# Filter layer 2, inverse row transform and whitening in four 64x64 parts of the array, in pairs of banks

## The reference, cut to what matters

```python
x = whiten(x) * gamma + beta             # per pixel a 64x64 product
h = layer_norm(x) * g1 + b1              # LN1
xf = rfft2(h, axes=(1, 2), norm='ortho') # 56 x 29 frequencies
o1 = relu(xf (complex) * w1 + b1)        # block diagonal, 8 blocks of 8: filter layer 1
o2 = softshrink(o1 (complex) * w2 + b2)  # filter layer 2, then shrink by 0.01
h = irfft2(o2) + h_input                 # inverse row transform, inverse column transform
y = gelu(layer_norm(h) @ mw1 + mb1) @ mw2 + mb2 + h    # LN2 and MLP, hidden 256
```

## Time and profile before

| | |
|---|---|
| median of the runs | 790.2 us (789.82 to 791.2) |
| the profiled execution's own time | 792.25 us |
| its span (first to last instruction) | 790.5 us |
| busy PE / DVE / ACT / POOL | 736.1 / 566.4 / 390.5 / 287.0 us |
| mean granted TensorE clock | 0.981 of full speed |
| one step in the middle (441.3 to 520.2 us) | 78.9 us |

### The profile page before, as it was taken

How to read it: one execution, slowest core, us unless ns; L and a number is a source line. 1 busy time by engine, 2 the same in 40 slices (tenths; PEclk the granted TensorE clock), 3 DMA queues, 4 the chain that set the end, 5 groups by cost and what they waited for, 6 DMA issues and landing times.

```text
span 790.5 us, 24576 instructions
## 1 busy us (share of the span) xinstructions
PE 736.1 (93%) x10489; PEld 495.7 (63%) x10489; DVE 566.4 (72%) x1845; ACT 390.5 (49%) x709; POOL 287.0 (36%) x158
## 2 busy tenths in 40 slices
PE   6988999788789999999999999999999999899887
PEld 5986557666566667666766677567766666557333
DVE  4566998869978587858785878587858794942741
ACT  0012004643746564656465646564656445645365
POOL 7000000771763356235623562356235624552000
PEclk9898999999999999999999999999999999989999
DMA  9974000203000400040004000300000000001001
GB/s 242 245 173 145 3 2 19 68 2 83 3 2 25 118 27 2 27 115 27 2 29 114 26 3 30 111 27 6 30 27 26 8 31 25 26 14 34 22 32 66
DMA packets 11069, 39.83 MB, mean 50 GB/s; under 512 B 1954, under 2 KB 2082, under 8 KB 9506
## 3 DMA queue, kind: packets, MB, share of 16 engines
q1 hardware_dynamic: 10962, 38.27, 17.1%
HBM read 25.42 MB, written 12.85 MB: 48 GB/s over the span
## 4 chain that ended last, share of the span: by engine, by line
PE 74%; DVE 17%; ACT 5%; issue 3%; DMA 0%; ACTq 0%; DVEq 0%
PE psum L1192 11%; PE psum L1183 10%; PE psum L1120 7%; PE psum L1131 6%; PE psum L1160 5%; PE psum L880 4%; PE psum L1047 4%; PE psum L1087 3%; DVE stats L626 3%; ACT o_g L1363 3%; PE psum L1173 3%; PE psum L931 3%; PE psum L1201 3%; DVE n L671 3%; PE psum L1104 3%
## 5 line engine op out<-in xcount | busy, mean ns | idle before, releaser
L1386 ACT ACTIVATE hid<-psum,hbias 128x448 f32<-128x448 f32 x224 | 123.9, 635 | 78.6 <-PE psum L1183 78.6
L459 POOL TENSOR_TENSOR p_y<-layer,clamped 128x512 f32<-128x512 f32 x64 | 75.9, 1186 | 90.9 <-DVE clamped L733 90.9
L438 POOL TENSOR_TENSOR hbuf<-hbuf,prm 128x896 f32<-128x896 f32 (+1 forms) x29 | 53.5, 1847 | 148.2 <-PE psum L1071 148.2
L1183 PE MATMUL psum<-n2T,mw1s 64*128 64x448 f32 x448 | 103.0, 577 | 3.0 <-ACT o_g L1363 2.2
L1192 PE MATMUL psum<-hid,prm 128*64 128x448 f32 x448 | 96.3, 552 | 3.3 <-DVE oslice L742 3.2
L433 POOL TENSOR_TENSOR rbuf<-ybuf,prm 128x512 f32<-128x512 f32 (+2 forms) x10 | 32.5, 3246 | 157.2 <-DVE hbuf L852 129.1
L727 DVE TENSOR_TENSOR layer<-psum,prm 128x512 f32<-128x512 f32 x64 | 40.4, 631 | 41.0 <-PE psum L1120 41.0
L1120 PEld LDWEIGHTS psum<-w2s,o_g 128*64 128x64 f32 x1856 | 60.1, 138 | 15.3 <-issue 11.2
L1131 PEld LDWEIGHTS psum<-cst,p_y 128*128 128x128 f32 x512 | 61.2, 192 | 10.6 <-issue 6.3
L1120 PE MATMUL psum<-w2s,o_g 128*64 128x64 f32 x1856 | 66.1, 224 | 1.6 <-ACT o_g L1363 1.2
L1131 PE MATMUL psum<-cst,p_y 128*128 128x112 f32 x512 | 66.6, 277 | 0.5 <-DVE layer L727 0.5
(11 more groups left out here) (138 smaller groups left out, 1338.0 us busy)
## 6 DMA issues: line engine op xcount, KB each, us to landing
xin<-x_dram SPq DMA_DIRECT2D x8, 1568.0 KB, 8.7
out_dram<-oslice SPq DMA_DIRECT2D x112, 112.0 KB
ybuf<-x_dram SPq DMA_DIRECT2D x2, 1568.0 KB, 18.4
fbuf<-x_dram SPq DMA_DIRECT2D x2, 1568.0 KB, 21.5
xin<-x_dram SPq DMA_DIRECT2D x4, 392.0 KB, 5.6
n<-x_dram SPq DMA_DIRECT2D x1, 1568.0 KB, 26.2
n<-x_dram SPq DMA_DIRECT2D x4, 392.0 KB, 18.9
prm<-params_dram SPq DMA_DIRECT2D x1, 742.0 KB, 4.1
```

The lines of the kernel that those rows point to most:

```text
L459: nc.gpsimd.tensor_tensor(yk, a, b, ALU.subtract).then_inc(y_ready, 1)
L1183: nc.tensor.matmul(t[:, 0:4 * ROWS], mw1s[C * v:C * v + C, HH * m:HH * m + HH], n2T[C * v:C * v + C, s % 2, :], start=True, stop=True).the ...
L1386: nc.scalar.activation(hid[:, s % 2, m, v, :], bank[CH_MLP[i].bank[k]][:, 0:4 * ROWS], ACT.Gelu, bias=hbias[:, m:m + 1]).then_inc(c_act, 1)
```

## The change

1. `layer_2`: instead of 128 input rows, each product takes the 64 rows of one image and 64 of the 128 outputs; one call fills two banks (one for each image, `b`) for `L2_KH[k]` frequency rows: 64, 64, 64 and 40 instructions. A pair still has 116 products. Before, a chunk was one half of the frequencies of both images in a bank; now the partition halves of a bank are the halves of the frequencies. The weights `w2s`, `mask2`, `fb2` shrink accordingly. POOL reads and writes chunks in the new arrangement.
2. `inv_w`: each product takes the 58 rows of half the channels (`h`) and 64 columns of weights; the real and imaginary halves (`s`) are accumulated: 8 products of 112 columns where there were 2, 256 instructions a pair. A call fills two banks, and it waits for all eight chunks (`y_ready` 8) where the first four calls waited for four.
3. `whiten_two(i, q)`: chunks 1+2, 3+4, 5+6 of pairs 2 to 7 in four parts, 64 columns each: 64 instructions for two chunks, where there were 16. `ev_whiten` writes every second column group.
4. Order on PE: slice 0 becomes `mlp_in` first half, `whiten_two(1)`, `mlp_in` second half, `transpose_n(1)`, `whiten_two(2)`. Slices 1 to 4 have five places; two chunks of layer 2 stand together. The last `inv_w` moves behind `mlp_in(5)`, `inv_h(0)` behind `dft_h(0)`, and `inv_h(3)` ahead of `dft_h(2)`.
5. Order on DVE: `multiply_rstd(i-1,1)` moves from ahead of the whitening evictions to behind them; layer 2 chunks are emptied two at a time, statistics in between; `ln2_stats` 0 and 1 move ahead of `ev_inv_h` 4 and 5. Order on ACT: the same five places, `ev_inv_w` two at a time.

```diff
-X_BESIDE = {1: [[0], [], [1], []], 2: [[2], [], [3], []], 3: [[4], [5], [6], []]}
+X_BESIDE = {1: [0, 1], 2: [2, 3], 3: [4, 5, 6]}
...
-                    if behind:
-                        multiply_rstd(i - 1, 1)
                     whitened_next(0, 1, 2)
...
+                    def second_product():
+                        if behind:
+                            multiply_rstd(i - 1, 1)
+
                     slice_(0, lambda: whitened_next(3, 4), lambda: whitened_next(5),
-                           lambda: whitened_next(6), lambda: stats_next(0))
-                    slice_(1, lambda: ev_layer_2(i, [0]), lambda: (ev_layer_2(i, [1]), stats_next(1)),
-                           lambda: ev_layer_2(i, [2]), lambda: (ev_layer_2(i, [3]), stats_next(2)))
-                    slice_(2, lambda: (ev_layer_2(i, [4]), stats_next(3)),
-                           lambda: (ev_layer_2(i, [5]), stats_next(4)),
-                           lambda: ev_layer_2(i, [6]), lambda: (ev_layer_2(i, [7]), stats_next(5)))
+                           lambda: whitened_next(6), second_product)
+                    slice_(1, lambda: ev_layer_2(i, [0, 1]), lambda: stats_next(0),
+                           lambda: ev_layer_2(i, [2, 3]), lambda: stats_next(1, 2))
+                    slice_(2, lambda: ev_layer_2(i, [4, 5]), lambda: stats_next(3),
+                           lambda: ev_layer_2(i, [6, 7]), lambda: stats_next(4, 5))
...
+                def whiten_two(i, q):
...
+                    for j in range(8):
+                        at = (4 + 8 * q + j) * RP
+                        for b in range(2):
+                            for v in range(2):
+                                rows = slice(C * v, C * v + C)
+                                last = nc.tensor.matmul(bank[WHITEN[2 * q + 1 + v]][C * b:C * b + C, j * C:j * C + C],
+                                                        xT[rows, at + C * b:at + C * b + C], wy[rows, rows], start=True, stop=True)
...
+                def layer_2(i, k, js):
+                    if k == 0 and i < PAIRS - 1:
+                        pe.wait_ge(whitened, (i + 1) * 7 + 6)
+                    t = [free_b(i, L2 + 2 * k + b) for b in range(2)]
+                    for j in js:
+                        for half in range(2):
+                            at = (half * KF + 8 * k + j) * KR
+                            for b in range(2):
+                                one = nc.tensor.matmul(t[b][C * half:C * half + C, j * C:j * C + C], o_g[C * b:C * b + C, at:at + C],
+                                                       w2s[C * b:C * b + C, C * half:C * half + C], start=True, stop=True)
...
+                def inv_w(i, k, js):
+
+                    pe.wait_ge(y_ready, i * 8 + 8)
+                    t = [free_b(i, INVW + 2 * k + h) for h in range(2)]
+                    for j in js:
+                        for s in range(2):
+                            for d in range(2):
+                                for h in range(2):
+                                    rows = slice(C * h, C * h + KR)
+                                    one = nc.tensor.matmul(t[h][C * d:C * d + C, j * 112:j * 112 + 112],
+                                                           y_v[rows, CH // 2 * s + 4 * k + j, C * d:C * d + C],
+                                                           cc("invw")[rows, 112 * s:112 * s + 112],
+                                                           start=(s == 0), stop=(s == 1), skip_group_check=True)
...
+                    def spectral_slice(s, one, two, three, four, five):
+
+                        if behind:
+                            mlp_in(i - 1, s)
+                        one()
+                        if behind:
+                            mlp_out(i - 1, s - 1)
+                        two()
+                        three()
+                        if behind:
+                            transpose_n(i - 1, s + 1)
+                        four()
+                        five()
+                        if behind:
+                            turn_out(i - 1, s - 1)
...
-                    slice_(0, whiten_next)
-                    slice_(1, and_x(1, lambda j: layer_2(i, j)))
-                    slice_(2, and_x(2, lambda j: layer_2(i, 4 + j)))
-                    slice_(3, and_x(3, lambda j: inv_w(i, [j])))
-                    slice_(4, lambda j: inv_w(i, [4 + j]))
+                    if behind:
+                        mlp_in(i - 1, 0, (0,))
+                    whiten_next(1)
+                    if behind:
+                        mlp_in(i - 1, 0, (1,))
+                        transpose_n(i - 1, 1)
+                    whiten_next(2)
+                    for s in (1, 2):
+                        a, b = 2 * s - 2, 2 * s - 1
+                        mid = L2_KH[b] // 2
+                        spectral_slice(s, lambda: layer_2(i, a, range(L2_KH[a])), lambda: x_next(X_BESIDE[s][0]),
+                                       lambda: layer_2(i, b, range(mid)), lambda: layer_2(i, b, range(mid, L2_KH[b])),
+                                       lambda: x_next(X_BESIDE[s][1]))
+                    spectral_slice(3, lambda: x_next(4), lambda: x_next(5), lambda: inv_w(i, 0, range(2)),
+                                   lambda: inv_w(i, 0, range(2, 4)), lambda: x_next(6))
+                    spectral_slice(4, lambda: inv_w(i, 1, range(4)), lambda: None, lambda: inv_w(i, 2, range(2)),
+                                   lambda: inv_w(i, 2, range(2, 4)), lambda: None)
```

More of the change, by code:

```diff
@@ L1109, in layer_1 @@
                                     one.then_inc(pe_b, 1)
-                def layer_2(i, c):
-                    half, k = c // 4, c % 4
-                    if c < 2 and i < PAIRS - 1:
-                        pe.wait_ge(whitened, (i + 1) * 7 + 5 + c)
-                    t = free_b(i, L2 + c)
-                    for j in range(L2_KH[k]):
-                        at = (half * KF + 8 * k + j) * KR
-                        for r in range(2):
-                            last = nc.tensor.matmul(t[C * r:C * r + C, j * C:j * C + C], o_g[:, at:at + C],
-                                                    w2s[:, 128 * half + C * r:128 * half + C * r + C],
-                                                    start=True, stop=True)
-                    last.then_inc(pe_b, 1)
@@ L1125, in inv_w @@
-                def inv_w(i, ks):
-                    for k in ks:
-                        pe.wait_ge(y_ready, i * 8 + 4 * (k // 4) + 4)
-                        t = free_b(i, INVW + k)
-                        for j in range(4):
-                            last = nc.tensor.matmul(t[:, j * 112:j * 112 + 112], y_v[:, 4 * k + j, :], cc("invw"),
-                                                    start=True, stop=True)
-                        last.then_inc(pe_b, 1)
+                def layer_2(i, k, js):
[8 more added lines that the diff above has]
+                                                       w2s[C * b:C * b + C, C * half:C * half + C], start=True, stop=True)
+                                if j == L2_KH[k] - 1 and half == 1:
+                                    one.then_inc(pe_b, 1)
@@ new lines, in inv_w @@
+                def inv_w(i, k, js):
[10 more added lines that the diff above has]
+                                                           start=(s == 0), stop=(s == 1), skip_group_check=True)
+                                    if j == 3 and s == 1 and d == 1:
+                                        one.then_inc(pe_b, 1)
@@ L1174, in transpose_n, with mlp_in @@
                     last.then_inc(pe_c, 1)
-                def mlp_in(i, s):
+                def mlp_in(i, s, ms=(0, 1)):
                     if s == SLICES - 1 and i + 2 < PAIRS:
@@ L1270, in step @@
                     mlp_in(i - 1, 5)
-                    inv_h(i, 0)
+                    inv_w(i, 3, range(4))
                     mlp_out(i - 1, 4)
@@ L1288, in step @@
                     else:
+                        transpose_n(i - 1, 6)
+                        inv_h(i, 0)
+                        turn_out(i - 1, 4)
+                        inv_h(i, 1)
+                        mlp_in(i - 1, 6)
+                        inv_h(i, 2)
+                        mlp_out(i - 1, 5)
                         turn_out(i - 1, 5)
@@ L1548, in constants @@
     put("mask1", m1.reshape(128, -1))
-    m2 = np.zeros((2, 2, CH, 2, 2, CH))
-    for b in range(2):
-        for r in range(2):
-            m2[b, r, :, 0, b] = same * (1.0 if r == 0 else -1.0)
-            m2[b, r, :, 1, b] = same
+    m2 = np.zeros((2, 2, CH, 2, CH))
+    for r in range(2):
+        m2[:, r, :, 0] = same * (1.0 if r == 0 else -1.0)
+        m2[:, r, :, 1] = same
     put("mask2", m2[..., L2_OUT].reshape(128, -1))
```

134 lines of the change are left out of this document (73 added, 61 removed).

## The result

The changed kernel takes **778.4 us** (776.18 to 779.6, 4 runs) against 790.0 for the kernel before on the same chip (788.18 to 791.2): ratio 0.9856, 95% interval 0.9836 to 0.9876. It is faster by 1.4%, inside the range, and 5.4 us above the forecast of 773. The profiled execution took 779.6 us with a span of 777.8; PE's mean granted clock fell from 0.981 to 0.966.

What follows compares the result with a forecast made beforehand. PE's issue order bounds a step until the DVE's milestones come late. Steps 1 to 5 save 17.0 us, step 6 1.8, step 7 2.6, step 0 loses 4.0: 17.4 off 792.25, 774.9; median 2.05 lower, 773; range 756 to 786.

Steps and rivals of the forecast that it cites:

- The prices in four parts: PE: `layer_2` and whitening 17.1 ns an instruction, `inv_w` 27; saving 3.6 us a pair, 2.6 a step, 0.8 a pair.
- Rival 4: `inv_w`: four-part products of 112 columns don't overlap four at a time; at 45 ns 810 us, slower; chance 0.06.
- If PE stayed the bound, a middle step would save 7.0.: Middle step: PE savings of layer 2, whitening and `inv_w` summed, 3.6 + 2.6 + 0.8 = 7.0 us.
- the third rival: Everywhere: bank-pair stalls, mode changes, `inv_w` at 35 ns; each step saves 1.3 us less, 784 us; chance 0.17.
- The DVE takes over.: Middle steps: the DVE's late milestones make PE wait, step 75.6 us; the forecast itself, 773 us; chance 0.50.
- the 3.3 us: Middle step: saving forecast from replaying the DVE's milestones, a step of 75.6 us, instead of PE's 7.0.
- rival 2: Middle steps: PE stays the bound, clamps don't stretch, a step saves 5.7 to 7.0 us; 758 us; chance 0.23.
- I take 4.0 lost: Step 0: `inv_w` starts later, calls and evictions alternate; last `inv_h` ends 3.9 us later, 4.0 us taken as lost.
- another 1 to 3: Step 0: further us lost if PE's clock falls in the gaps, for example after the thin stretch before 181 us.
- Step 7 and the last MLP: Layer 2 and `inv_w` save 4.4 us, bank pairs take 0.3 back, later LN2 loses 1.5: net 2.6.
- The moved product: Second LN2 product behind the whitening costs 2.0 us instead of 3.25; `mlp_in(1)` starts at 461.0 instead of 463.55, 2.5 gained.

Runs made afterwards that it cites:

- the kernel with spread statistics: Kernel after, with LN1 statistics put between bias add and clamp of every second layer 2 chunk, the third part moved further back: 770.8 us.
- The whole calls: Kernel after, with each slice's second `layer_2` call and two `inv_w` calls no longer split around a transpose: 784.5 us.
- with step 0 mended as well: Kernel after, with LN1 statistics spread, banks 4 to 7 for step 0's second and third `inv_w` calls, and useless products filling PE's waits: 765.0 us.
- the one with banks and filling: Kernel after, with banks 4 to 7 for step 0's second and third `inv_w` calls and useless products filling PE's waits before `inv_w`: 771.4 us.

## Why the prediction was right, and where it was not

- **The prices in four parts.** Right: 17.0 ns for `layer_2` and whitening, 26.4 ns in a whole call of `inv_w` (forecast 17.1, 17.1 and 27). `layer_2` saved 3.5 us (3.6), whitening 2.3 (2.6: a call of before took 1.90 on the average of the step, not the 1.95 of the one row, and a new one 1.13, not 1.09), `inv_w` 0.34 (0.8). The last was mis-sized on the side of before: its calls cost 7.50 us, not the 7.75 of one row times 64, and half calls now cost 0.93 where half of a whole one is 0.85. Rival 4 is out. The rows held against it were misread, though: the earlier trace rows are three products of 128 columns beside one of 65 (L945, not shown there), not four of 128.
- **"If PE stayed the bound, a middle step would save 7.0."** Wrong: 4.9, as the kernel with spread statistics shows (its 74.0 us still hold the waits for ACT). The three products saved 6.1, `inv_h` took 0.1 more, and two terms were left out: the neighbours, 1.75 us in the 36 pieces of MLP and transposes, and the new wait of 0.80 for ACT (0.86 for the DVE went in exchange). That belongs to the third rival, which had it together with bank stalls at 1.3 us. (By its own terms that rival saves 5.1 to 5.5 us and not 6.0, which gives 785 and not 784.)
- **Where the neighbours pay.** By arrangement I mean the rows and columns of the array that a product takes (64 or 128 each, 56 and 58 counted as 64, 112 as 128). Where no wait follows, a transpose of four instructions takes 0.39 to 0.44 us from start to start if the next piece has the same arrangement and 0.53 to 0.59 (once 0.71) if it has another, in both kernels (465.56 to 466.00 and 464.35 to 464.94 above), and `mlp_out` before took 1.55 and 1.65. In the step before, the arrangement changes at 47 of 69 borders between pieces, in the step after at 62 of 67: 15 more for 1.75 us, about 0.12 each. That is read off the traces; no experiment changes the borders alone. The whole calls come nearest: 7 borders less, 0.66 us less in the products and 0.30 more in the neighbours, three of which then stood ahead of a wait. The Trainium skill, "TensorEngine Tiling (Array Packing)", section "Tiling Modes", says that changing the tiling mode drains the engine, without a price; the direction agrees with these rows.
- **"The DVE takes over."** Right in its places and nearly in its times. Counted from `dft_w`, the third chunk pair's banks came free at 34.2 us (forecast 34.0), `mlp_out` of slice 4 could start at 48.3 (48.7), and 27.2 us of PE work followed (26.9): 75.4 against 75.6. The second clamp of each pair cost 1.00 or 1.01 three times a step and 0.69 the fourth, 2.1 us more in all than the first clamps (forecast 2.2), the product 2.02. The Trainium skill, "SBUF — State Buffer", section "Who interferes with whom", names a lock that VectorE and GpSimd share; the clamp at 0.41 once the statistics stand between agrees.
- **So the 3.3 us came out for half a reason, and in part by luck.** The DVE's milestones were the forecast's, but PE came to the first of them 0.6 us later (33.2 against 32.6 us from `dft_w`) and waited 1.3 us for the DVE in all, in place of 3.1. The work that the sum of PE left out fell where PE would have waited anyway. Had the DVE been free, as in rival 2, a step would have saved 4.9 and not 5.7 to 7.0; with the DVE's waits gone the kernel takes 770.8 us and not rival 2's 758, and with step 0 mended as well 765.
- **Step 0.** The step that failed is "I take 4.0 lost": it was 8.8 us, or 8.3 measured from the first `layer_2`. The places were right (`inv_w` at 181.0, waits of 1.15 between calls, `inv_h` at 195.7 where 192.8 was forecast). The 2.9 us between are the clock at 0.50 under the first two calls, 1.5 us each, which the text had as "another 1 to 3" and left out of the sum; and of the 8.25 us by which `inv_h` begins later than before, 1.4 were to be hidden by the DVE, and 0.3 was. This step makes up the whole miss of the profiled execution: 4.8 us, where the profiled execution, 779.6, lies 4.7 above the 774.9 forecast for it; the other differences cancel (step 7 +1.7, steps 1 to 6 -0.9, the part ahead of step 0 -0.9). How the small differences fall is of this one execution, as step 1 shows.
- **Step 7 and the last MLP.** Forecast 2.6, measured 0.9, by two errors. `layer_2` and `inv_w` saved 3.1 (7.57 to 4.78 and 7.46 to 7.12), not 4.4, and the neighbours and waits took 2 back (waits 6.21 to 7.15 us). The 1.5 us lost at the end did not come: from `turn_out` at 735.9 to the end of the span are 41.9 us, before it were 41.9 too. PE waits 1.82 us at 738.37, and the clock falls there (0.50 from 740 to 745) instead of at 760. That account is read off the two traces; no experiment stands behind it.
- **The moved product.** Right in what it gives at the whitening: `mlp_in(1)` starts at 458.56 - 438.41 = 20.15 us after `dft_w`, 19.7 forecast, 22.2 before. Too small in what hangs on it: with the product ahead, a middle step is as long as before (78.9 us), and the four-part products bring nothing there.

## What to carry to other kernels

Read where the bound engine arrives and where the next one is ready as two separate lists of times: the step follows the later of each pair, so a wrong sum of work can hide behind a right milestone. A product made faster is worth its saving only if what it waits for is moved ahead of it or what it hid is hidden anew; here the order on VectorE was worth 3.5 us a step, and the split calls 0.6 to 0.9. And where TensorE idles in two stretches behind each other, mend both before judging either, since the clock that falls in one is not seen in the other.

## What the runs showed of the hardware that I had not expected

- In the kernel with the product ahead, a wait of 2.06 us of TensorE cost another 1.6 us through the granted clock of 0.53 in the 3.6 us behind it. Waits of 1.06 us in dense work cost nothing more (clock 1.00).
- Which stretch the lower clock meets differs between executions of nearly the same program. From 150 to 158 us, where nothing was changed, it was 0.69 and 0.50 in the kernel after and 1.00 in the one with banks and filling; from the first `dft_w` to the first `layer_2` that is 17.3 against 15.2 us. Single times of one kernel lie up to 10 us apart (780.7 to 790.7 with whole calls), more than those of the kernel before on the same chip (786.3 to 792.8).
- Unchanged work beside the four-part products took 1.75 us more in a step of 75 us. A transpose of 0.44 us took 0.53 to 0.59 where the piece behind it had another arrangement of the array, and each further piece into which a four-part product is cut cost 0.16 us in that product.
